# One graph layer: the inverse roots' Newton rounds move from GpSimd to VectorE, and nodes follow edges at 18 steps

## The reference

```python
h = jnp.maximum(_layernorm(x, axis=-1), 0.0)
msg_input = jnp.concatenate([h[src], h[dst]], axis=1)
# per edge, with the weights of its type t:
m = jax.nn.relu(msg_input @ W1[t] + b1[t]) @ W2[t] + b2[t]
agg = jax.ops.segment_sum(msgs, dst, num_segments=num_nodes)
gi = agg @ W_ih.T + b_ih
gh = h @ W_hh.T + b_hh
r = sigmoid(i_r + h_r); z = sigmoid(i_z + h_z)
n = jnp.tanh(i_n + r * h_n)
out = x + (1.0 - z) * n + z * h
```

## Time and profile before

| what | us |
|---|---|
| median of 3 runs | 1767.15 |
| the profiled execution | 1767.82 |
| its span, first to last instruction | 1765.9 |
| TensorE busy in the span | 1627.0 |
| VectorE busy | 1598.9 |
| GpSimd busy | 1227.6 |

### The profile page before, as it was taken

The page is one execution under the profiler, slowest core; times in us unless marked ns, Lnnn a source line. Parts: engine busy times, 40 slices in busy tenths (PEclk is TensorE's granted clock), DMA queues, the critical chain, the costliest instruction groups (busy, mean ns, idle before and its releaser), DMA issues.

```text
span 1765.9 us, 43091 instructions
## 1 busy us (share of the span) xinstructions
PE 1627.0 (92%) x10182; PEld 1429.8 (81%) x10182; DVE 1598.9 (91%) x4185; ACT 1457.9 (83%) x3401; POOL 1227.6 (70%) x1974
## 2 busy tenths in 40 slices
PE   0236899999999999999999999999999999999998
PEld 0225788888888888888888888888888888888886
DVE  8796799999999999999999999999999999999886
ACT  0035789898989999989999999999999999999895
POOL 5776787787777877777776767767667676676420
PEclk9999899999999999999999999999999999999999
DMA  2224677777777777777777777777777777777653
GB/s 74 56 60 132 159 199 200 203 199 199 202 194 199 202 198 202 195 200 195 196 200 199 195 199 195 198 195 198 196 200 194 200 194 200 196 195 199 182 140 98
DMA packets 476814, 319.57 MB, mean 181 GB/s; under 512 B 106577, under 2 KB 462881, under 8 KB 476706
## 3 DMA queue, kind: packets, MB, share of 16 engines
q10 hardware_dynamic: 261792, 156.12, 29.3%
q1 hardware_dynamic: 185730, 106.99, 25.8%
q0 software_dynamic: 29184, 55.33, 12.5%
HBM read 211.65 MB, written 106.58 MB: 180 GB/s over the span
## 4 chain that ended last, share of the span: by engine, by line
PE 88%; ACT 1%; issue 1%; POOL 0%; DVE 0%; DVEq 0%; POOLq 0%; ACTq 0%
PE bank L1352 17%; PE bank L1354 15%; PE bank L1353 15%; PE bank L1432 11%; PE bank L1444 5%; PE bank L1443 5%; PE bank L1460 5%; PE bank L1422 5%; PE bank L1470 5%; PE bank L1414 5%; PE bank L1456 1%; POOL e_x L592 0%; ACT n_zc L1305 0%; DVE n_sel L1091 0%; DVE n_out L1077 0%
## 5 line engine op out<-in xcount | busy, mean ns | idle before, releaser
L592 POOL DMA_INDIRECT e_x<-in_x,rows_now x816 | 850.6, 1042 | 236.2 <-issue 221.5
L1197 ACT ACTIVATE e_h<-e_x,shift,rstd 128x128 f32<-128x128 f32 x816 | 355.5, 486 | 107.7 <-DVE shift L1068 83.7
L1214 ACT ACTIVATE n_h<-n_x,shift,rstd 128x128 f32<-128x128 f32 x784 | 385.4, 492 | 0.0
L1352 PE MATMUL bank<-n_h_hi,whh_hi 128*128 128x512 f32 x588 | 248.1, 422 | 2.5 <-ACT n_zc L1305 2.1
L1352 PE MATMUL bank<-n_a_hi,wih_hi 128*128 128x512 f32 x588 | 248.9, 423 | 0.9 <-DVE bank L1103 0.9
L1091 DVE TENSOR_SCALAR n_sel<-iota,n_rel 128x256 fp32r<-128x256 f32 x784 | 239.6, 368 | 8.1 <-POOL n_rel L643 6.7
L1432 PE MATMUL bank<-n_sel,n_win 128*128 128x256 f32 x1568 | 234.4, 292 | 9.9 <-DVE n_sel L1091 9.9
L1354 PE MATMUL bank<-n_a_hi,wih_lo 128*128 128x512 f32 x588 | 232.5, 395 | 0.0
L1353 PE MATMUL bank<-n_h_lo,whh_hi 128*128 128x512 f32 x588 | 232.5, 395 | 0.0
L1354 PE MATMUL bank<-n_h_hi,whh_lo 128*128 128x512 f32 x588 | 232.3, 395 | 0.0
L1353 PE MATMUL bank<-n_a_lo,wih_hi 128*128 128x512 f32 x588 | 231.9, 394 | 0.0
(11 more groups left out here) (181 smaller groups left out, 3759.9 us busy)
## 6 DMA issues: line engine op xcount, KB each, us to landing
n_win<-messages SPq DMA_DIRECT2D x1568, 64.2 KB
messages<-e_msg ACTq DMA_DIRECT2D x204, 257.0 KB, 2.9
n_x<-in_x ACTq DMA_DIRECT2D x195, 256.0 KB
out<-n_out ACTq DMA_DIRECT2D x195, 256.0 KB, 2.3
e_x<-in_x,rows_now POOLq DMA_INDIRECT x816
rows_now<-lists SPq DMA_DIRECT2D x204, 2.0 KB, 3.0
lists<-picks,list_rows POOLq DMA_INDIRECT x72, 2.5
w<-in_W SPq DMA_DIRECT2D x1, 512.0 KB, 4.9
```

The lines of the kernel that those rows point to most:

```text
L592: G.indirect_dma_start(e_x[:, s, 2 * end + t, :], None, x, bass.IndirectOffsetOnAxis(ap=rows_now[:, s, t, end:end + 1], axis=0)).then_inc( ...
L1197: last = A.activation(e_h[:, s % 2, k, :], e_x[:, s, k, :], ACT.Relu, scale=rstd[:, slot, col + k:col + k + 1], bias=shift[:, slot, col + ...
L1214: last = A.activation(n_h[:, s % 2, cols], n_x[:, s, cols], ACT.Relu, scale=rstd[:, slot, col + 4 + k:col + 5 + k], bias=shift[:, slot, co ...
L1352: T.matmul(o, w_hi, v_hi, start=start, stop=False, skip_group_check=onto)
```

## The change

All 12 Newton instructions become VectorE's (`newton`): the first 8 stand at places 0 to 7 of the step with m % 4 = 1, the next four at places 0, 1 and 2 (two of them) of the step after. The subtraction from a tile of 1.5 becomes a multiply and add with constants. GpSimd's function goes.

`LAG` becomes 18 and `AHEAD` 5, so that a group waits for units up to g + 5; both together leave the distance between a store and the load that waits for it as it was. In the head, the wait for `ranked` moves from step 1 to step 3, the fetch by ranks from step 3 to step 5, `find_starts` from step 5 to step 7, and the starts' transfers from step 7 to step 9. The fetch uses a table in DRAM that holds destinations and types side by side, written by two new transfers at the start, so that 4 indirect DMAs do what 8 did. In steps before 16 `low_half` stands behind the statistics instead of at the step's start. The lists' halves are written from step 20.

```diff
-LAG = 20
-AHEAD = 7
+LAG = 18
+AHEAD = 5
...
-WRITE_FROM = 16
+WRITE_FROM = 20
...
+            sp.dma_start(ends_types[:, 0, :], dst_flat[0:EROWS].rearrange("(c p) -> c p", p=P)).then_inc(s_table, 16)
+            sp.dma_start(ends_types[:, 1, :], types[0, :].rearrange("(c p) -> c p", p=P)).then_inc(s_table, 16)
...
-                inverse_roots(i, m)
-                if isinstance(i, int) and i == 3:
+                if isinstance(i, int) and i == 5:
                     pool.wait_ge(s_rank_i, 1)
+                    pool.wait_ge(s_table, 32)
                     for b in range(4):
-                        for k, table in enumerate((dst_flat[0:EROWS], types[0, :])):
-                            G.indirect_dma_start(found[:, k, b, :], None, table.rearrange("(c p) -> c p", p=P),
-                                                 bass.IndirectOffsetOnAxis(ap=rank_i[:, b:b + 1], axis=0)
-                                                 ).then_inc(s_found, 16)
+                        G.indirect_dma_start(found[:, b].rearrange("p k c -> p (k c)"), None,
+                                             ends_types.rearrange("c k p -> c (k p)"),
+                                             bass.IndirectOffsetOnAxis(ap=rank_i[:, b:b + 1], axis=0)).then_inc(s_found, 16)
...
+            def newton(first, n, slot):
+                dve.wait_ge(ln_ops, first * (LN_ROOTS // 4) + n + 1)
+                old, new = ((root, root2), (root2, root), (root, rstd[:, slot, :]))[n // 4]
+                if n % 4 == 0:
+                    ins = V.tensor_tensor(root_t[:], old[:], old[:], ALU.mult)
+                elif n % 4 == 1:
+                    ins = V.tensor_tensor(root_u[:], root_t[:], half_var[:], ALU.mult)
+                elif n % 4 == 2:
+                    ins = V.tensor_scalar(root_t[:], root_u[:], -1.0, 1.5, ALU.mult, ALU.add)
+                elif n < 11:
+                    ins = V.tensor_tensor(new[:], root_t[:], old[:], ALU.mult)
+                else:
...
+                    V.tensor_tensor(new, root_t[:], old[:], ALU.mult).then_inc(ln_rooted, 4)
+                    return
+                ins.then_inc(ln_ops, 1)
...
+                elif third == 1:
+                    newton(first, place, slot)
+                elif third == 2 and place < 3:
+                    newton(first, 8 + place, slot)
+                    if place == 2:
+                        newton(first, 11, slot)
...
+                in_head = isinstance(i, int) and i < LAG - 2
+                if not in_head:
+                    low_half(i, m)
...
+                if in_head:
+                    low_half(i, m)
...
+                if isinstance(i, int) and i == 3:
+                    take_ranks()
+                if isinstance(i, int) and i == 7:
                     find_starts()
```

More of the change, by code:

```diff
@@ L42 @@
 SPAN = (1 << 12) - 1
-WRITE_FROM = 16
+WRITE_FROM = 20
 WRITE_EVERY = 4
-WRITE_HEAD = 112
+WRITE_HEAD = 120
 LIST_HEAD = 128
@@ L109, in gnn_layer @@
     starts_dram = nc.dram_tensor("starts", (P * 16,), I32, kind="Internal").ap()
+    ends_types = nc.dram_tensor("ends_types", (ECOLS, 2, P), I32, kind="Internal").ap()
     ctx = ExitStack()
@@ L229, in gnn_layer @@
         bound_line = borrow(n_x[:], (SEGMENTS + 1) * 4 * P, 4 * P)
[L230 to L231 removed]
+        found = n_t[:].rearrange("p r w -> p (r w)").bitcast(I32).rearrange("p (b k c) -> p b k c", b=4, k=2)
+        found_f = n_n[:].rearrange("p r w -> p (r w)").rearrange("p (b k c) -> p b k c", b=4, k=2)
         smaller = borrow(n_zc[:], 0, 4 * P).rearrange("p (b c) -> p b c", b=4)
@@ L320, in gnn_layer @@
         s_found = sem("s_found")
+        s_table = sem("s_table")
         s_starts_i = sem("s_starts_i")
@@ L369, in gnn_layer @@
         ln_vared = sem("ln_vared")
-        ln_seeded = sem("ln_seeded")
         ln_ops = sem("ln_ops")
@@ L476, in starts_and_general @@
             def starts_and_general(i):
-                if i == 7:
+                if i == 9:
                     sp.wait_ge(s_starts_i, 1)
@@ L645, in relative_tags @@
                                 base[:, bass.ds(2 * g, 2)].unsqueeze(2).to_broadcast([P, 2, 2]), ALU.add).then_inc(n_reled, 1)
[L647 to L670, removed]
             def half_of(i):
@@ L888, in rank_bounds, with take_ranks @@
                 ins.then_inc(s_passed, 1)
+            def take_ranks():
                 dve.wait_ge(s_ranked, 1)
@@ L898, in find_starts @@
             def find_starts():
-                dve.wait_ge(s_found, 16 * 8)
+                dve.wait_ge(s_found, 16 * 4)
                 link(V.tensor_copy(found_f, found))
-                link(V.tensor_tensor(smaller, found_f[:, 0], bound[:].unsqueeze(2).to_broadcast([P, 4, P]), ALU.is_lt))
+                link(V.tensor_tensor(smaller, found_f[:, :, 0], bound[:].unsqueeze(2).to_broadcast([P, 4, P]), ALU.is_lt))
                 for t in range(TYPES):
-                    link(V.scalar_tensor_tensor(out=mine, in0=found_f[:, 1], scalar=float(t), in1=smaller,
+                    link(V.scalar_tensor_tensor(out=mine, in0=found_f[:, :, 1], scalar=float(t), in1=smaller,
                                                 op0=ALU.is_equal, op1=ALU.mult))
@@ L1044, in node_stats @@
                 return last
+            def newton(first, n, slot):
[10 more added lines that the diff above has]
+                else:
+                    if due(first - 4):
+                        dve.wait_ge(e_normed, first - 4)
+                    if due(first - LAG + 5):
+                        dve.wait_ge(n_normed, first - LAG + 5)
+                    V.tensor_tensor(new, root_t[:], old[:], ALU.mult).then_inc(ln_rooted, 4)
+                    return
+                ins.then_inc(ln_ops, 1)
             def ln_part(i, m, place):
@@ L1069, in ln_part, with low_half @@
                                            op0=ALU.mult, op1=ALU.mult).then_inc(ln_shifted, 4)
+            def low_half(i, m):
+                q, s = i - 10, (m - 10) % UNROLL
+                if within(q, UNITS):
+                    dve.wait_ge(e_high, q + 1)
+                    V.tensor_tensor(e_msg[:, s, :, D:2 * D],
+                                    bank[BE1][:, message_part].rearrange("p (t d) -> p t d", t=2),
+                                    e_msg[:, s, :, 0:D].bitcast(F32), ALU.subtract).then_inc(e_low, 1)
             def step(i, m):
@@ L1151, in step @@
                     rank_bounds()
-                if isinstance(i, int) and i == 5:
+                if isinstance(i, int) and i == 3:
+                    take_ranks()
+                if isinstance(i, int) and i == 7:
                     find_starts()
```

4 lines of the change are left out of this document (1 added, 3 removed).

## The result

The changed kernel takes 1747.05 us, the median of 4 runs (1746.99 to 1749.81), against 1767.7 for the kernel before beside it: a ratio of 0.9886, 95% interval 0.9871 to 0.9901. It is faster by 20.7 us. Spans and rows are those of the profiled executions, 1746.99 us after and 1767.82 before.

What follows compares the result with a forecast made beforehand. It took TensorE, busy without a gap, to bound the loop and the head to decide where the loop starts. From 1767.82: -15.8 (head) + 3.1 (end) + 1.0 (loop) = 1756.1, forecast 1756 us, range 1749 to 1768.

Steps and rivals of the forecast that it cites:

- The step that failed: Loop: TensorE never stops, so VectorE's gains there are worth nothing and the loop cannot get faster; forecast +1.0 us.
- The price of the rounds in the loop: Loop: VectorE's added Newton instructions are almost hidden, 0.02 us a batch, 49 batches, 1 us.
- the cover: Loop, step with eight Newton instructions: waits of 0.78 us together hide the 0.70 us added to VectorE's line.
- My sign that `n_out` still ends before the weight load: Loop: `n_out`, which ended 0.07 us ahead of TensorE's weight load that needs it, would still end before it.
- The second rival: Loop: VectorE becomes the bound, each Newton instruction costing its whole 0.19 us in line; 27 us, 1782; chance 0.12.
- The head: Start to first window sum: first group asks for units 0 to 5, not 7; sum at 167.9, 15.8 us earlier.
- VectorE's sum: Head, VectorE's time up to step 15's `e_low`: -8.7 + 6.2 + 1.4 + 1.4 = +0.3 us.
- the other three terms: Head, VectorE: wait for `ranked` gone, -8.7; node statistics two steps earlier, +1.4; `e_low` behind both statistics pairs, +1.4.
- the third rival: First three steps up to 2 us faster with TensorE less idle, head 3 us sooner with cheaper chained rounds; 1751; chance 0.11.
- The end: Last steps: two steps with nodes alone become full steps, 16.06 us instead of 12.93, giving back 3.1 us.
- the general path: Check of the starts fails with `AHEAD` 5, so a path taking many times as long runs; chance 0.01.

Runs made afterwards that it cites:

- tile_back: The changed kernel with the 128-byte tile of 1.5 put back, unread, in its old place in SBUF; 1753.3 us.
- twice: The changed kernel with a second small unread instruction behind each Newton instruction of the loop, from step 64 on; 1778.09 us (one run).
- gpsimd_roots_last: The changed kernel with Newton rounds on GpSimd again and the tile of 1.5 declared last, so node tiles keep their changed places; 1739.77 us.
- vector_roots: The kernel before with only the Newton rounds moved to VectorE, and so without the tile of 1.5; 1764.08 us, ratio 0.9979.
- old_distance: The changed kernel with `LAG` 20 and `AHEAD` 7 as before the change; 1757.42 us.
- gpsimd_roots: The changed kernel with Newton rounds on GpSimd again and the tile of 1.5 in its old place; 1750.8 us.
- edges_moved: gpsimd_roots_last with the edge tiles 128 bytes higher, node tiles and weights where they were; 1740.52 us.

## Why the prediction was wrong

**The step that failed** is the loop's: "below nothing it cannot go, since TensorE has no gap to give." A busy TensorE is not one at its fastest. The interval of its gates' matmuls had 0.0026 us to give, 18 times a step. I priced the instructions that the change adds and removes, but not the tile that it removes: with GpSimd's function `three_halves` goes, the tiles declared behind it move by 128 bytes, and I gave that no term at all. With GpSimd's roots, the distance alone is worth 4.54 us in 96 steps (769.31 less 764.77), 8.9 us over 189; with VectorE's it is worth 3.47 (769.93 less 766.46), 6.8 us.

**The price of the rounds in the loop** was right where I measured the cover: at distance 192, 0.62 us in 96 steps, 0.026 a batch against my 0.02. With a faster TensorE there is less cover: the waits for `n_out` grow from 3.0 us (tile_back) to 8.8, and the price became 0.07 (1.69 over 24 batches). My sign that `n_out` still ends before the weight load did not hold, with 42 waits. So the loop's net of -4.8 us is about -8.9 for the distance and +3.3 for VectorE's rounds (1.69 x 189 / 96), or -6.8 and +1.2 if the rounds are counted first. Of the remaining 0.8, some 0.7 lies in the 93 steps outside the 96, and is not explained. The second rival, VectorE as the bound, supposed that an instruction costs its whole 0.19 us of the line; over the loop, 12 of them take 1.50 us from each one's start to the next start, 0.125 on average and below the 0.15 from which that rival decides. That VectorE can become the bound, twice shows, with 12 more. In the changed kernel's loop:

```profile
1004.39 0.18 DVE L1033 TENSOR_TENSOR root<-root_t,root 128x32 f32<-128x32 f32 x1
1004.49 0.68 DVE L1088 TENSOR_TENSOR n_out<-n_xh,bank 128x512 f32<-128x512 f32 x1
```

It lasts 0.18 us and waits on VectorE's own semaphore, and the next starts after 0.10. The Trainium skill's page "VectorE: DVE Perf Modes" (The DRAIN you can't avoid) has the next operation start when the pipeline is empty; read as a rule, that would have each instruction cost its 0.18. The same paragraph says that a next operation which is not held (made to wait for the earlier ones) starts earlier, and this pair agrees with that, at 0.10.

**The head** was right in its sum and in its chain: `e_low` at 154.09 (154.4 said), windows at 157.00 (158.2), first window sum at 166.70 (167.9). SyncE came 2.5 us behind the store instead of 3.4, which is most of the 1.2. The last window landed some 3 us behind the end of its issue, as assumed. That VectorE's sum came out within 0.3 us is in part luck: the 36 Newton instructions up to step 14 take 7.0 us, each from its start to the next start, where I had 6.2, so the other three terms gave 0 - 7.0 = -7.0, not the -5.9 of my sum, and two errors of about 1 us cancelled. Without VectorE's rounds the same `e_low` of gpsimd_roots_last starts only 4.1 us earlier, because there VectorE waits 2.74 us for gathered rows:

```profile
88.24 0.76 DVE L1033 BATCH_NORM_STATS2 bn<-e_x 128x6 f32<-128x256 f32 x2 [2.74 <-DMA e_x<-in_x,rows_now]
...
150.00 0.40 DVE L1101 TENSOR_TENSOR e_msg<-bank,e_msg 128x256 fp32r<-128x256 f32 x1
```

Taken one by one, moving the roots costs the first window sum 1.9 us (before to vector_roots), the head's changes win 8.5 (to old_distance), the distance of 18 steps wins 10.4 (to after).

**The stretch behind the first window sum** was 1.4 us shorter, as the third rival said of an idle TensorE. The sum itself still took 2.08 us. What also changed is the granted clock (columns after the stretch: busy time of PE, PEld, DVE, ACT, POOL; the clock is the third number from the right), before and after:

```profile
150.00:200.00 50.00, 31.36 (x151) 27.24 (x152) 24.21 (x81) 28.77 (x70) 36.33 (x56) 0.80 0.53 138
```

```profile
150.00:200.00 50.00, 42.76 (x237) 37.00 (x238) 37.07 (x117) 39.37 (x94) 31.09 (x40) 1.00 0.65 172
```

At 0.80 the mean lies between the two levels of 1.2 and 2.4 GHz; at 1.00 it is 2.4 throughout. (The kernel before is not at 9 tenths or more in all of the page's slices: the fifth, which this stretch overlaps, has 8.) TensorE idled 8.97 us ahead of its first sum before and 0.48 after. That idle time or clock is the cause is not shown, and two kernels speak against it: tile_back, with 1.66 us of idle time and a clock of 1.00 from its first sum to its first closing at 190.35, needs 22.98 us for that; gpsimd_roots_last, at a clock of 0.91 there, needs 21.18, as the changed kernel does. old_distance needs 20.46. So 1.4 us is within what kernels that differ in other things differ by here, and this part of the third rival stays open.

**The end** gave back 2.4 us where I had 3.1. The time leaves no room for the general path.

## What to carry to other kernels

- A full share of busy time is no floor. Before writing that a bound engine can gain nothing, compare the interval of its instructions with the same instructions in another kernel, or with their tiles at another place.
- An edit that adds or removes a tile moves every tile behind it. Here 128 bytes moved the time by 6 us (tile_back against after) to 11 us (gpsimd_roots against gpsimd_roots_last), and hid that the move of the roots, the edit in the title, lost time by itself. Keep the places fixed when you compare two kernels, and try a few distances when you tune.
- A cover (idle time that hides added work) worked out at one pace shrinks when the engine that gave it gets faster: the same 12 instructions cost 0.026 us a batch at one pace and 0.07 at the other.

## What the runs showed of the hardware

In this loop the start of a matmul with 512 streamed columns follows the one before by 0.2301 to 0.2309 us where streamed operand and weights lie 64 bytes apart modulo 256 (twice, with its waits, left out), 0.2311 at 0, 0.2326 at 128 and 0.2330 to 0.2334 at 192. The Trainium skill's page "SBUF — State Buffer" (A bandwidth-pool intuition that's wrong) gives TensorE a second, independent read port for weight loads; by that the distance should not matter. The runs show that it does, by about 1%. What in the memory makes it so, and which distances between these four are good, they do not tell.

GpSimd's Newton instructions beside VectorE and TensorE cost the loop nothing that shows: 764.77 us for 96 steps is the shortest of all but edges_moved, its equal, and the steps with them are no longer than those without.
